# The last chunk of a DLRM tower finished in two parts of two tiles

## The reference

```
e = stack([tbl_f[ids[:, f]] for f in range(26)], axis=1)
sd = einsum('bfd,bd->bf', e, dense);  ss = einsum('bfd,bgd->bfg', e, e)
z = concatenate([dense, sd, ss[:, iu, ju]], axis=1)      # iu, ju: triu_indices(26, k=1)
h = concatenate([z, dense], axis=1)
h = maximum(h @ W_top1 + b_top1, 0)      # 607 -> 512
h = maximum(h @ W_top2 + b_top2, 0)      # 512 -> 256
y = h @ W_top3                           # 256 -> 1
```

## Time and profile before

| | |
|---|---|
| median of 3 runs | 396.62 us (396.27 to 397.1) |
| profiled execution | 395.68 us |
| its span | 393.9 us |
| busy share | PE 87%, PEld 67%, POOL 69%, DVE 61%, ACT 46% |
| granted TensorE clock, mean | 0.965 |
| last gather issued | 354.30 us into the span |

### The profile page before, as it was taken

One profiled execution on the slowest core, in us unless ns is written; L12 is line 12 of the kernel. 1 busy time (PEld: TensorE's weight loads), 2 busy tenths in 40 slices (PEclk: granted clock), 3 DMA queues, 4 the chain that ended last, 5 costly groups with the idle time before them and its releaser, 6 DMA issues.

```text
span 393.9 us, 12374 instructions
## 1 busy us (share of the span) xinstructions
PE 344.1 (87%) x5434; PEld 262.5 (67%) x5434; DVE 240.8 (61%) x466; ACT 182.5 (46%) x280; POOL 270.6 (69%) x279
## 2 busy tenths in 40 slices
PE   5799977887999998798999998799999988545996
PEld 1566655765788875586788875687788865435773
DVE  1799993685898643686998642588997541101420
ACT  3544155783223227775223338575133258932333
POOL 6788887777777777777777777777777777770000
PEclk9999996999999999999999999899999999958899
DMA  7995113243343223343333214243333122110000
GB/s 193 258 260 144 40 42 116 66 108 81 78 109 87 55 53 76 96 116 85 96 97 87 53 47 123 59 115 84 108 80 85 53 61 56 52 55 17 2 2 0
DMA packets 20089, 33.41 MB, mean 85 GB/s; under 512 B 7907, under 2 KB 10467, under 8 KB 20037
## 3 DMA queue, kind: packets, MB, share of 16 engines
q0 software_dynamic: 8704, 17.84, 18.0%
q1 hardware_dynamic: 11333, 14.78, 14.0%
HBM read 32.60 MB, written 0.01 MB: 83 GB/s over the span
## 4 chain that ended last, share of the span: by engine, by line
PE 45%; POOL 34%; issue 14%; DMA 3%; ACT 2%; DVE 1%; POOLq 0%; ACTq 0%; DVEq 0%
POOL rows L440 34%; PE late_bank L533 9%; PE gram_bank L500 7%; PE late_bank L461 6%; PE late_bank L462 5%; PE turn_bank L481 5%; PE turn_bank L461 3%; PE turn_bank L462 3%; DMA rows<-in_tbl_dram,index 2%; PE spare_bank L567 2%; PE gram_bank L567 1%; PE late_bank L578 1%; ACT turned L324 1%; PE turn_bank L514 1%; PE gram_bank L514 1%
## 5 line engine op out<-in xcount | busy, mean ns | idle before, releaser
L440 POOL DMA_INDIRECT rows<-in_tbl_dram,index x272 | 269.8, 992 | 84.1 <-issue 80.8
L803 DVE TENSOR_TENSOR one_hot<-table_ids,row_number 125x512 fp32r<-125x512 int32 x216 | 133.7, 681 | 24.9 <-PE turn_bank L462 15.6
L324 ACT COPY turned<-turn_bank 128x512 f32<-128x512 f32 (+1 forms) x72 | 70.6, 1029 | 43.8 <-PE turn_bank L481 39.6
L461 PE MATMUL late_bank<-one_hot,table_hi 125*128 125x512 f32 x192 | 81.0, 422 | 3.8 <-DVE table_lo L875 3.4
L462 PE MATMUL late_bank<-one_hot,table_lo 125*128 125x512 f32 x192 | 76.7, 399 | 0.0
L481 PE MATMUL turn_bank<-ident,rows 128*128 128x128 f32 x288 | 47.5, 298 | 23.7 <-DMA rows<-in_tbl_dram,index 13.7
L500 PE MATMUL gram_bank<-turned 128*27 128x26 f32 x4096 | 55.1, 195 | 13.3 <-issue 13.0
L500 PEld LDWEIGHTS gram_bank<-turned 128*27 128x27 f32 x4096 | 45.6, 108 | 29.7 <-issue 27.4
L481 PEld LDWEIGHTS turn_bank<-ident,rows 128*128 128x128 f32 x288 | 35.0, 151 | 35.5 <-issue 16.1
L295 DVE COPY gram<-gram_bank 124x208 f32<-124x208 f32 x32 | 12.0, 374 | 69.9 <-PE gram_bank L500 69.8
L461 PEld LDWEIGHTS late_bank<-one_hot,table_hi 125*128 125x128 f32 x192 | 36.6, 191 | 17.0 <-DVE table_lo L875 5.0
(11 more groups left out here) (74 smaller groups left out, 327.6 us busy)
## 6 DMA issues: line engine op xcount, KB each, us to landing
table_ids<-in_ids_by_table_dram SPq DMA_DIRECT2D x27, 256.0 KB, 3.3
rows<-in_tbl_dram,index POOLq DMA_INDIRECT x272
turned<-in_tbl_dram SPq DMA_DIRECT2D x6, 448.0 KB, 11.7
looked_up<-in_tbl_dram SPq DMA_DIRECT2D x3, 448.0 KB, 5.1
rows<-in_r_dense_features_dram SPq DMA_DIRECT2D x16, 64.0 KB, 2.8
gram<-in_W_top_dram SPq DMA_DIRECT2D x1, 702.0 KB
gram<-in_W_top_dram SPq DMA_DIRECT2D x1, 512.0 KB
turned<-in_tbl_dram SPq DMA_DIRECT2D x6, 52.0 KB
```

Of the source, the lines that this page charges most:

```text
L324: copy(to[:, f0:f1], of).then_inc(rows_copied[n % 2], 1)
L440: pool.indirect_dma_start(out=rows[:, row % RING_ROWS, :], out_offset=None, in_=tables[f], in_offset=bass.IndirectOffsetOnAxis(ap=index[:, ...
L461: pe.matmul(bank, table_hi[:, s, k, :], hot, start=k == 0, stop=False)
L803: last = nc.vector.tensor_tensor(hot, table_ids[0:RK, (c * LOOKUPS + s) % ID_SLOTS, :], row_number[0:RK, k:k + 1].broadcast_to([RK, CHUNK] ...
```

## The change

The function calls after the loop over tiles become `finish_part`, on PE, ACT and DVE alike, and take a `part` instead of a chunk. The first three chunks have one part of four tiles, as before. The last chunk has two parts: tiles 0 and 1, and tiles 2 and 3. After tile 1's products PE, ACT and DVE finish the first part; then come the products of tiles 2 and 3 and the second part. In each part the column transposes give 64 instead of 128 partitions and the pairs, layers and activations have 256 instead of 512 columns. The first part's pairs lie in `gram`, in the place of the products of tiles 2 and 3. The column transposes wait in addition until tile 2's turned rows are copied, since they use the same banks. There is one more store, and the counts in the waits follow.

```diff
+Part = namedtuple("Part", "n chunk first end")
+def parts_of(chunk, chunks):
+    if chunk < chunks - 1:
+        return [Part(chunk, chunk, 0, TILES)]
+    return [Part(chunk, chunk, 0, TILES // 2), Part(chunk + 1, chunk, TILES // 2, TILES)]
+def samples_of(part):
+    return slice(part.first * P, part.end * P)
+def groups_in(part):
+    return (part.end - part.first) * GROUPS
...
+        late_pairs = turned[:, (TILES - 1) % 2].rearrange("p i f -> p (i f)")[:, 0:GROUP * PAIRS]
+        early_pairs = late_room[:, TILES // 2 * GROUPS * LATER:TILES // 2 * GROUPS * LATER + GROUP * PAIRS]
...
+        def pairs_of(part):
+            room = late_pairs if part.end == TILES else early_pairs
+            return room[0:groups_in(part)].rearrange("p (q f) -> p q f", q=GROUP)
...
+                engine.wait_ge(dense_split, (part.chunk + 1) * TILES + part.end)
+            engine.wait_ge(cols_turned, part.n * COLS_TURNS + g + 1)
             for i in range(g * TURN, min((g + 1) * TURN, LATER)):
-                of = cols_bank[g][:, i % TURN * P:(i % TURN + 1) * P].rearrange("p (q f) -> p q f", q=GROUP)
-                last = copy(pairs[:, :, offset(i):offset(i + 1)], of[:, :, i + 1:FEATURES])
+                of = cols_bank[g][0:groups_in(part), i % TURN * P:(i % TURN + 1) * P].rearrange("p (q f) -> p q f", q=GROUP)
+                last = copy(pairs_of(part)[:, :, offset(i):offset(i + 1)], of[:, :, i + 1:FEATURES])
             last.then_inc(cols_copied[g % 2], 1)
...
+            def store(part):
+                sp.wait_ge(y_copied, part.n + 2)
+                sp.dma_start(out[part.chunk * CHUNK:(part.chunk + 1) * CHUNK][samples_of(part), :].rearrange("b n -> n b"),
+                             y[:, samples_of(part)]).then_inc(stored, DMA)
...
+                store(parts_of(c - 1, chunks)[0])
+            for part in parts_of(chunks - 1, chunks):
+                store(part)
+            sp.wait_ge(stored, (chunks + 2) * DMA)
...
+                        pe.wait_ge(gram_copied[i], (part.chunk + 1) * (ALL_UNITS // 2) + part.end * UNITS // 2)
+                    wait_all_rows(pe, part.chunk * ALL_TURNS + min(part.end + 1, TILES) * TURNS)
                 if g >= COLS_TURNS - 2:
-                    pe.wait_ge(cols_copied[0], c * COLS_STEPS[0] + g - (COLS_TURNS - 2) + 1)
+                    pe.wait_ge(cols_copied[0], part.n * COLS_STEPS[0] + g - (COLS_TURNS - 2) + 1)
+                groups = slice(part.first * GROUPS, part.end * GROUPS)
                 for i in range(g * TURN, min((g + 1) * TURN, LATER)):
-                    last = pe.transpose(cols_bank[g][:, i % TURN * P:i % TURN * P + ACROSS], gram[0:ACROSS, :, i],
-                                        ident[0:ACROSS, 0:ACROSS])
+                    last = pe.transpose(cols_bank[g][0:groups_in(part), i % TURN * P:i % TURN * P + ACROSS],
+                                        gram[0:ACROSS, groups, i], ident[0:ACROSS, 0:ACROSS])
                 last.then_inc(cols_turned, 1)
...
+                high = groups_in(part)
+                to = pairs_bank[k][0:PK, samples_of(part)].rearrange("p (t q i) -> p q t i", q=GROUP, i=GROUPS)
                 for q in range(GROUP):
-                    last = pe.transpose(to[:, q], pairs[:, q, k * PK:(k + 1) * PK], ident[:])
+                    last = pe.transpose(to[:, q], pairs_of(part)[:, q, k * PK:(k + 1) * PK], ident[0:high, 0:high])
                 last.then_inc(pairs_turned, 1)
...
+                p, cols, samples = height(k), slice(n * P, (n + 1) * P), samples_of(part)
                 for w, x in ((w1_hi, input_hi), (w1_hi, input_lo), (w1_lo, input_hi)):
-                    last = pe.matmul(h1_bank[n], w[0:p, k, cols], x[0:p, k, :],
+                    last = pe.matmul(h1_bank[n][:, samples], w[0:p, k, cols], x[0:p, k, samples],
                                      start=k == 0 and x is input_hi and w is w1_hi, stop=k == K1 - 1 and w is w1_lo)
...
+                        last = pe.matmul(h2_bank[n][:, samples], w[:, k, n * P:(n + 1) * P], x[:, k % H1_SLOTS, samples],
...
+            def finish_part(part, more):
+                c = part.chunk
+                dense_ahead(part, 0, more)
                 for g in range(COLS_TURNS):
-                    turn_products(c, g)
+                    turn_products(part, g)
                     if more:
                         if g == COLS_TURNS - 1:
-                            pe.wait_ge(cols_copied[1], c * COLS_STEPS[1] + 1)
+                            pe.wait_ge(cols_copied[1], part.n * COLS_STEPS[1] + 1)
                         look_up(c + 1, blocks_after("columns", g))
                 for k in range(K_PAIRS):
-                    turn_pairs(c, k)
+                    turn_pairs(part, k)
                     if more:
                         look_up(c + 1, blocks_after("pairs", k))
-                dense_ahead(c, 1, more)
+                dense_ahead(part, 1, more)
                 for n in range(N1):
-                    layer1(c, n)
+                    layer1(part, n)
                     if more:
                         look_up(c + 1, blocks_after("layer1", n))
                     for k in LAYER2_AFTER[n]:
-                        layer2(c, k)
+                        layer2(part, k)
                 if more:
                     turn_rows(c + 1, 0, range(0, 2))
-                layer2(c, N1 - 1)
+                layer2(part, N1 - 1)
                 if more:
                     turn_rows(c + 1, 0, range(2, TURNS))
-                layer3(c)
+                layer3(part)
...
+            def work_off(c, more):
+                for part in parts_of(c, chunks):
+                    for t in range(part.first, part.end):
+                        awaited = not more and t == TILES - 2
+                        for u in range(UNITS):
+                            if t + 1 < TILES:
+                                turn_rows(c, t + 1, turns_before(u, awaited))
+                            products(c, t, u)
+                            if more:
+                                if blocks_before(("unit", t, u)) == 0:
+                                    pe.wait_ge(y_copied, c + 1)
+                                look_up(c + 1, blocks_after("unit", t, u))
+                        if awaited:
+                            turn_rows(c, t + 1, turns_before(UNITS, awaited))
+                    finish_part(part, more)
...
+            def relu1(part, n):
...
+                for to, made in ((h1_hi[:, n % H1_SLOTS, samples], h1_hi_made), (h1_bank[n][:, samples], h1_made)):
+                    nc.scalar.activation(to, h1_bank[n][:, samples], ACT.Relu, bias=b1_sb[:, n:n + 1]).then_inc(made, 1)
...
+            def copy_output(part):
+                act.wait_ge(y_summed, part.n + 1)
+                nc.scalar.copy(y[:, samples_of(part)], y_bank[:, samples_of(part)]).then_inc(y_copied, 1)
...
```

193 lines of the change are left out of this document (88 added, 105 removed).

## The result

| | before | after |
|---|---|---|
| median of 20 runs | 396.19 us (394.37 to 398.15) | 398.00 us (395.86 to 402.36) |
| ratio | | 1.0045, interval 1.0024 to 1.0066 |
| profiled execution, its span | 395.68, 393.9 us | 400.19, 398.0 us |
| granted clock, mean | 0.965 | 0.961 |

The changed kernel is 1.8 us slower, where 0.5 us faster was forecast. Its fastest run has a span of 393.7 us, close to the 393.4 forecast; the median does not. Its runs also spread over 6.5 us where those of before spread over 3.8, and the profiled one is 2.2 us above its median.

What follows compares the result with a forecast made beforehand. Gathers, then PE alone for about 37 us, bound the end. Columns starting at 375.2 plus 3.35 + 1.6 + 10.85 + 2.4 gave a span of 393.4 us against 393.9, median 396.1; range 392.8 to 400.5.

Steps and rivals of the forecast that it cites:

- The order in time: Last chunk's schedule: first part starts at 342.05 us, tile 3's products end at 374.85, the span ends at 393.4.
- products of tiles 2 and 3: PE between the two parts: 16.35 us, with waits for ACT's turn copies and 3.29 us of gaps in tile 3.
- second part's columns: PE after tile 3: 26 transposes of 0.115 us, 3.0, plus 0.35 for last copy and hand-over, 3.35 us.
- layers: Each part, up to the copy of y: 60 matmuls of 0.127 us, 7.6, plus waits, 10.85 us together.
- what it overruns pushes the products: Wait for gathers holds about 8 us of idle PE; the first part needs more, and the excess delays later products.
- a lower clock: PE in either part's finish: named as a sign the forecast is wrong; clock 1.0 expected from 342 to 358 us.
- the dense matmuls run beside it: Behind tile 3's products: three dense matmuls overlap ACT's copy of 0.35 us, so columns start at 375.2.
- 256-column prices: Both parts' finishes: layer matmuls 0.127 us apart, copies and activations 0.42 us on DVE, 0.39 to 0.40 on ACT.
- rival of dear 256 columns: Layer matmuls in both parts cost more than half: 402.5 us at 0.188 each, 408 at 0.233; chance 0.12.
- rival of a filled buffer: PE has its instructions in time for tiles 2 and 3, gaps of 3.3 and 0.6 us go: 392.2 us; chance 0.24.
- rival of slower instructions: Instruction packets for PE 3.8 us apart, 15.7 us for tiles 2 and 3's products; 398.1 us; chance 0.20.
- trailing gap: One more PE gap of 2 us before the end, if the first crossing finds no instruction packet ahead.

Runs made afterwards that it cites:

- two runs with idle work: Four unused matmuls, 3.4 us on PE, put behind tile 1's products of the last chunk: before 397.16 us, ratio 0.9994; the changed kernel 401.97 us, ratio 1.0101.
- held: The changed kernel with POOL holding the last eleven gathers until tile 1's products of the last chunk are done: 399.88 us, ratio to before 1.0088.
- filled run: The changed kernel with four unused matmuls among the last tile's products: 646.02 us, ratio 1.0124, on a chip where before takes 641.32 us.
- before held: The kernel before with POOL holding the last eleven gathers until tile 1's products of the last chunk are done: 397.26 us, ratio 1.0036.
- spread version: The changed kernel with most of the first part's layer matmuls issued in small groups behind the units of tiles 2 and 3: 390.85 us, ratio to before 0.9830.

## Why the prediction was wrong

Range and rough shape held, the side did not. The step that failed is the start of the first part in "The order in time": "The first part starts at 342.05". From the profiled execution's 393.4 forecast to 398.0 measured:

| step | forecast | measured | difference |
|---|---|---|---|
| first part starts | 342.05 | 345.51 | +3.5 |
| first part, to PE free | 16.45 | 16.5 | 0 |
| products of tiles 2 and 3 | 16.35 | 15.7 | -0.6 |
| dense matmuls to columns | 0.35 | 0.94 | +0.6 |
| second part's columns | 3.35 | 4.85 | +1.5 |
| pairs | 1.6 | 1.8 | +0.2 |
| layers | 10.85 | 10.84 | 0 |
| copy of y, store | 2.4 | 1.84 | -0.6 |

- *The start.* I took 342.05 from one execution as given. In before little hangs on it: the last gather is issued at 354.30, and PE waits for gathers for 7.6 us, which is slack for what comes late just ahead of them. The change spends this slack. No row of before shows a cost for it, only the wait itself; the question to put was what else the wait was absorbing. The two runs with idle work show it: 0 against 2.2 us or more of 3.4. (It does not absorb all: by my estimate from the last gathers, 1.75 of this profile's 3.5 us would have come through in before as well.) I counted only that "what it overruns pushes the products"; that the start itself might come later had no term, and none of my rivals had it.
- *The second part's columns.* I named a lower clock as what would make me wrong, but gave it no price and no chance. Yet before had it at this very place: its three dense matmuls took 1.65 us behind the gap, which I left out of "the dense matmuls run beside it" without a reason. Here the gaps are as long, and the windows read 0.81 and 0.62. The held and the filled run show the same columns at 1.00 in 3.24 and 3.22 us. So it is the dip, 1.5 us in columns and up to 0.6 in the dense matmuls ahead. It is not the change's own: eight columns in 1.65 us stand in before held and in the changed kernel alike, in the changed kernel with idle work they took 1.57, and in the changed kernel held 0.97.
- *Right:* the 256-column prices. Forecast spacing 0.127, measured 0.118. The Trainium skill (TensorE: Matmul & The Clock Gate, "Back-to-back issue gap") has 262 cycles, 0.109 us, for the gap of a single matmul by itself. The trace lies between. DVE takes 0.42 as forecast, ACT 0.47 and 0.44 instead of 0.40. That the layers came out to 0.01 us is in part luck: at 0.118 sixty matmuls are 0.5 us cheaper than forecast, and the waits between them were that much dearer. The rival of dear 256 columns (0.145 and up) is refuted.
- *Right:* PE waits for ACT's turn copies in tile 2, 1.97 us, and tile 3's standstills stay, behind the 72nd and the 200th record, 128 apart. The rival of a filled buffer is refuted: 1.06, 0.87 and 2.64 us of standstill. The Trainium skill (Runtime: NRT & Kernel Launch, "Instruction fetch mechanics") has the fetch in blocks of 16 KB, or 256 instructions, and mostly hidden. The spacing of 128 matmul records, which with their 128 weight loads are 256 instructions, agrees with blocks; the 2.64 us don't agree with hidden. The rival of slower instructions had 15.7 us for both tiles, which is what came, but without its trailing gap: the 2.64 was the last. Its sum is also off: with its own 15.7 in place of 16.35 it comes to 397.5 and not 398.1. That 398.1 meets the measured median of 398.0 is luck, as is that the median lies in the stated range: start and clock were in no rival.

Of the 4.6 us between forecast and profile, 2.2 belong to this execution, which is that much above its median. How the 1.8 us of the medians divide between lateness and clock stays open, since one profile shows one execution of each kernel, and lateness itself came in part with a lower clock. Shown is that the changed kernel passes lateness on which before absorbs, and that the lower clock costs the second part 1.5 to 2.1 us where it comes. In the spread version's profile PE comes late as well, at 344.4, and the second part has the full clock.

## What to carry to other kernels

A wait for data is also slack for what comes late just ahead of it. Before filling it with work from behind, ask how much the arrival at it varies from run to run, and count that variation as cost. And when a block of work is moved into a wait, spread it between the small instructions there rather than in one piece: here nearly the same instructions cost 1.0045 of before as a block and 0.983 spread.

## What the runs showed of the hardware

- In the last tile's stream of small matmuls PE stands still for 0.5 to 2.6 us every 128 matmul records, at fixed places of its stream; where the clock was 0.50 the first of them was missing. Eight records added upstream (the idle work in before) brought the standstills eight records earlier in the tile, behind the 53rd and 181st. With 3.4 us of long matmuls among them the standstills vanish.
- Behind a tile with PE busy 3.05 of 6.56 us the granted clock fell to 0.62 over 5.75 us; over the same tile with PE busy 2.83 of 5.80 us it stayed at 1.00 in another execution. The dip is not decided by the kernel alone. In before it was 0.50 over the 2.07 us behind the gap.
- Chips differ more than kernels: on four of the six chips of the experiments every kernel took 629 to 678 us instead of some 396. In before's profile there the products of tile 12, with the turns between them, took 36.8 us and those of tiles 13 to 15, with all gathers issued, 5.3 to 7.1. What helps on one sort of chip (0.983) did nothing on the other (0.999).
